# A decoder layer on one core: expert results added in memory by accumulating transfers, a joint way back per tile, a reordered opening

## The reference, cut to what matters

```
x = layernorm(x + self_attention(x))                    # x: 16 x 56 x 256, 16 heads of 16
x = layernorm(x + cross_attention(x, ctx))              # ctx: 16 x 1500 x 256; int8-rounded q and output projections
def ffn(x):                                             # 896 tokens, 8 experts, 2 of them per token
    probs = softmax(x @ gate_w + gate_b)
    weights, selected = top_k(probs, 2); weights /= sum(weights)
    h = gelu(einsum('nd,edf->enf', x, w1) + b1); y = einsum('enf,efd->end', h, w2) + b2
    return einsum('ne,end->nd', comb, y)                # comb holds the two weights of a token
x = layernorm(x + ffn(x))
```

## Time and profile before

| | us |
|---|---|
| median of three runs | 987.98 |
| the profiled execution | 990.07 |
| its span, first to last instruction | 988.1 |

### The profile page before, as it was taken

One profiled execution on the slowest core, in us unless ns is written; L12 is line 12 of the kernel. 1 busy time (PEld: TensorE's weight loads), 2 busy tenths in 40 slices (PEclk: granted clock), 3 DMA queues, 4 the chain that ended last, 5 costly groups with the idle time before them and its releaser, 6 DMA issues.

```text
span 988.1 us, 29769 instructions
## 1 busy us (share of the span) xinstructions
PE 863.9 (87%) x12092; PEld 702.3 (71%) x12093; DVE 623.5 (63%) x1191; ACT 462.0 (47%) x1049; POOL 223.7 (23%) x185
## 2 busy tenths in 40 slices
PE   5759989999999999999999999999987299999950
PEld 3537877787778777777877777787765189988950
DVE  4647676968787877879797877979665411111115
ACT  2316655645565565556555655656554123322310
POOL 4123113212512422152223214222300100000026
PEclk9859999989999999999999999999997589999985
DMA  6424546454644645455455545555538154454523
GB/s 200 134 84 124 151 142 180 122 153 124 188 133 142 185 141 154 146 170 142 151 153 154 158 142 165 147 161 147 190 107 343 56 200 167 171 193 160 170 76 100
DMA packets 98102, 151.32 MB, mean 153 GB/s; under 512 B 12002, under 2 KB 86306, under 8 KB 94144
## 3 DMA queue, kind: packets, MB, share of 16 engines
q1 hardware_dynamic: 96448, 145.40, 47.9%
q0 software_dynamic: 1536, 4.20, 1.3%
HBM read 102.61 MB, written 46.86 MB: 151 GB/s over the span
## 4 chain that ended last, share of the span: by engine, by line
PE 56%; DVE 16%; DMA 11%; ACT 7%; issue 4%; SPq 3%; POOL 2%; DVEq 0%; ACTq 0%
PE ps L1283 9%; PE ps L1290 9%; PE ps L1349 6%; PE ps L1576 6%; PE ps L1588 5%; DVE negmax L445 5%; PE ps L1306 5%; DMA k_dram<-k_two 5%; PE ps L1329 5%; DMA w_sb<-w 3%; PE ps L1358 3%; ACT k_two L1099 3%; DVE k_two L439 2%; ACT pT L1126 2%; DMA k_st<-k_dram 2%
## 5 line engine op out<-in xcount | busy, mean ns | idle before, releaser
L445 DVE TENSOR_REDUCE negmax<-ps 112x1 f32<-112x1500 f32 x128 | 219.3, 1713 | 30.3 <-PE ps L1306 30.1
L1126 ACT ACTIVATE pT<-ps 125x448 f32<-125x448 f32 x384 | 195.5, 547 | 38.0 <-PE ps L1329 34.5
L977 POOL TENSOR_TENSOR ctx_lo<-ctx_raw,ctx_hi 128x1000 fp32r<-128x1000 f32 x47 | 109.7, 2335 | 240.0 <-DVE ctx_hi L430 240.0
L1329 PE MATMUL ps<-qbd,k_st 98*128 98x112 f16 x1536 | 127.4, 216 | 7.2 <-ACT pT L1126 3.6
L1329 PEld LDWEIGHTS ps<-qbd,k_st 98*128 98x128 f16 x1536 | 89.6, 100 | 58.6 <-issue 20.1
L439 DVE SCALAR_TENSOR_TENSOR k_two<-ps,bk_sb,k_two 128x500 f16<-128x500 f32 x96 | 70.8, 738 | 72.0 <-ACT k_two L1099 71.8
L1099 ACT ACTIVATE k_two<-ps,bk_sb 128x500 f16<-128x500 f32 x96 | 65.0, 677 | 89.2 <-PE ps L1283 70.7
L1306 PE MATMUL ps<-k_st,qbd 96*112 96x500 f16 x384 | 104.7, 381 | 0.0
L1082 ACT COPY v_sb<-ps 125x512 f32<-125x512 f32 x96 | 56.3, 586 | 97.9 <-PE ps L1290 97.9
L1237 ACT ACTIVATE hT<-ps,b_col 128x128 f32<-128x128 f32 x168 | 47.9, 368 | 115.2 <-PE ps L1576 115.2
L1349 PE MATMUL ps<-pT,v_sb 125*17 125x56 f32 x6144 | 95.0, 218 | 7.0 <-issue 7.0
(11 more groups left out here) (199 smaller groups left out, 1228.4 us busy)
## 6 DMA issues: line engine op xcount, KB each, us to landing
k_st<-k_dram SPq DMA_DIRECT2D x288, 125.0 KB, 2.6
w_sb<-w SPq DMA_DIRECT2D x29, 1024.0 KB, 4.9
ctx_raw<-ctx_T SPq DMA_DIRECT2D x48, 500.0 KB, 4.5
k_dram<-k_two SPq DMA_DIRECT2D x96, 250.0 KB, 3.4
xs<-zeros SPq DMA_DIRECT2D x28, 256.0 KB, 2.8
ys<-zeros SPq DMA_DIRECT2D x28, 256.0 KB, 2.7
xg<-xs SPq DMA_DIRECT2D x21, 128.0 KB, 4.0
ys<-y_sb SPq DMA_DIRECT2D x21, 128.0 KB, 1.7
```

The lines of the kernel that those rows point to most:

```text
L445: V.tensor_reduce(negmax[0:QW], ps[0:QW, BANK_S:BANK_S + CHUNKS, 0:MC], AX.XY, ALU.max, negate=True).then_inc(max_done, 1)
L977: nc.gpsimd.tensor_tensor(ctx_lo[:, k], ctx_raw[:, k], ctx_hi[:, k].bitcast(F32), ALU.subtract).then_inc(ctx_lo_done, 1)
L1126: nc.scalar.activation(pT[0:MT, (PAIRS * b + p) % 3, TPC * g:TPC * g + TPC], ps[0:MT, BANK_T + n % 2, 0:TPC * QW].rearrange("p (t n) -> p ...
L1329: last = mm(ps[:, BANK_T + n % 2, QW * i:QW * i + QW], k_st[:, j, p, a:a + P], qbd[:, j, p].rearrange("p h s -> p (h s)"), start=True, sto ...
```

## The change

Rows of `xs` become 260 wide: 256 values, then the token's number plus one, the exponential of the gap of its two best logits, and its best expert's number. Routing no longer computes gates or gather slots. x2 is written per tile into a new tensor `sums` (`keep_x2`), and `ys` and its zeroing are gone. In the expert loop VectorE reads the extra columns (`gate`: seven instructions per tile) for the gate, the destination row and b2 times gate; `y_step` gives gate times y plus that; POOL adds the 128 rows into `sums` by one indirect transfer with an add, each waiting for the one before. The row buffer is now reloaded after `gate` has read it, not after the transpose. At the end SP loads `sums` back in four pieces, and ACT normalises tiles 0 to 3, VectorE tiles 4 to 7.

The way back is made once per tile, for both of its batches together, at slot 2 of the even batch and after the last. In the opening the units are spread behind the steps by `FIRST_UNITS`, the last unit goes behind the first scores, the int8 rounding is cut into parts and moved behind steps 4, 7 and 12, wq and wp are loaded ahead of the second context chunk, and some constants move. `o_all` is no longer cleared.

```
-        x1_all = sb("x1_all", [P, TILES, D])
+        rows_all = sb("rows_all", [P, TILES, XW])
+        x1_all = rows_all[:, :, 0:D]
...
+        FIRST_UNITS = {0: (1,), 2: (2,), 4: (3, 4), 5: (5,), 7: (6,), 9: (7, 8), 12: (9,), 14: (10,)}
+        W_GRID, W_INT, W_SCALED = (2, 10), (6, 17), 17
...
-            def o_step(b, par, t):
...
+            def o_step(t):
+                dve.wait_ge(o_back_done, t + 1)
+                o = ps[:, BANK_O, 0:H * VW].rearrange("p (h d) -> p h d", d=VW)
+                V.reciprocal(rsum[:].unsqueeze(2), o[:, :, DH:VW]).then_inc(rsum_done, 1)
+                dve.wait_ge(rsum_done, t + 1)
+                V.tensor_tensor(o_all[:, t].rearrange("p (h d) -> p h d", h=H), o[:, :, 0:DH],
+                                rsum[:].unsqueeze(2).to_broadcast([P, H, DH]), ALU.mult).then_inc(o_read, 1)
+                dve.wait_ge(o_read, t + 1)
+                V.tensor_tensor(o_all[:, t], o_all[:, t], bv_b[:], ALU.add).then_inc(o_done, 1)
...
-                    dve.wait_ge(p_act, t + 1)
-                    V.tensor_scalar(r_den[:], r_exp[:], 1.0, None, ALU.add).then_inc(route, 1)
-                    dve.wait_ge(route, n + 14)
-                    V.reciprocal(comb[:, 0, t:t + 1], r_den[:]).then_inc(route, 1)
-                    dve.wait_ge(route, n + 15)
-                    V.tensor_tensor(comb[:, 1, t:t + 1], r_exp[:], comb[:, 0, t:t + 1], ALU.mult).then_inc(route, 1)
                     if t < TILES - 1:
                         V.tensor_tensor(ohsum[:], ohsum[:], oh16[:], ALU.add).then_inc(route, 1)
-                    dve.wait_ge(route, n + 16)
+                        dve.wait_ge(route, ROUTE * t + 14)
...
-                    elif slot == 2 and not (isinstance(b, int) and b == 0):
-                        o_step(b - 1, 1 - j, t - 1 + j)
+                    elif slot == 2 and b == 0:
+                        row_tails()
+                    elif slot == 2 and j == 0:
+                        o_step(t - 1)
...
+            unit_step(0, 0, 0)
             for k in range(A_STEPS):
-                if k < UNITS:
-                    unit_step(0, 0, k)
-                if k == 3:
-                    ctx_hi_step(0, 0, 2)
-                elif k == 8:
-                    ctx_hi_step(1, 1, 0)
                 a_step(k, 0)
                 a_tail(k, 0)
                 if k == 2:
                     kbd_part(0)
-                elif k == 3:
+                elif k == 4:
+                    ctx_hi_step(0, 0, 2)
+                    dve.wait_ge(w_nat_in, 32)
+                    weights_grid(0)
+                    weights_int8(0)
+                elif k == 7:
+                    weights_grid(1)
+                elif k == 10:
                     dve.wait_ge(small_in, 16 * len(SMALL))
-                    weights_to_int8(0)
-                elif k == 5:
-                    weights_to_int8(1)
-                elif k == 7:
+                elif k == 12:
+                    weights_int8(1)
+                elif k == 13:
+                    ctx_hi_step(1, 1, 0)
+                for u in FIRST_UNITS.get(9 if k == 10 else k if k != 9 else -1, ()):
+                    unit_step(0, 0, u)
             max_step(0, 0)
             row_halves(0, 0)
+            unit_step(0, 0, 11)
...
+            def gate(g):
+                row, q = xg[:, g % 2], g % 4
+                one = slice(q, q + 1)
+                e = dve.value_load(e_tab[0:1, g:g + 1], min_val=0, max_val=E - 1)
+                V.scalar_tensor_tensor(g_num[:, one], row[:, D + 2:D + 3], e_sum[:, g:g + 1], row[:, D + 1:D + 2],
+                                       ALU.is_equal, ALU.max).then_inc(gate_step, 1)
+                V.tensor_scalar(g_den[:, one], row[:, D + 1:D + 2], 1.0, None, ALU.add).then_inc(gate_step, 1)
+                V.tensor_scalar(g_spare[:, one], row[:, D:D + 1], 0.5, p_back[:, 2:3], ALU.is_lt, ALU.mult).then_inc(gate_step, 1)
+                dve.wait_ge(gate_step, 5 * g + 3)
+                V.scalar_tensor_tensor(g_token[:, one], row[:, D:D + 1], -1.0, g_spare[:, one], ALU.add, ALU.max).then_inc(row_read, 1)
+                V.reciprocal(g_rec[:, one], g_den[:, one]).then_inc(gate_step, 1)
+                dve.wait_ge(gate_step, 5 * g + 4)
+                V.tensor_tensor(g_gate[:, one], g_num[:, one], g_rec[:, one], ALU.mult).then_inc(gate_step, 1)
+                dve.wait_ge(gate_step, 5 * g + 5)
+                V.tensor_scalar(g_b2[:, q], b2_all[:, bass.ds(e, 1)].rearrange("p a n -> p (a n)"), g_gate[:, one], None,
+                                ALU.mult).then_inc(gate_done, 1)
+            def y_step(g):
+                q = g % 4
+                dve.wait_ge(gate_done, g + 1)
                 dve.wait_ge(m2_done, g + 1)
-                if not (isinstance(n, int) and n == 0):
-                    dve.wait_ge(y_out[par], 16 * n)
-                V.tensor_tensor(y_sb[:, par], ps[:, Y_BANK + par, 0:D], b2_all[:, bass.ds(e, 1)].rearrange("p a n -> p (a n)"),
-                                ALU.add).then_inc(y_ready, 1)
...
+            gate(0)
+            gate(1)
+            for g in range(GT):
+                if g + 2 < GT:
+                    xgT_step(g + 2, g % 2)
+                y_step(g)
+                if g + 2 < GT:
+                    gate(g + 2)
...
+            for half in range(2):
+                tiles = range(4 * half, 4 * half + 4)
+                for t in tiles:
+                    dve.wait_ge(sum_in[t // 2], 16)
+                    V.bn_stats(st8[:, t], acc[:, t]).then_inc(f_stat, 1)
...
+            for n, src in enumerate((wq, wp)):
+                sp.dma_start(w_nat[n], src[:]).then_inc(w_nat_in, 16)
             load_ctx(0, 0, 1, True)
             for dst, src in SMALL:
...
+            def keep_x2(t, kept):
+                sp.wait_ge(b_x2_kept, kept)
+                sp.dma_start(sums_tiles[bass.ds(t, 1)].rearrange("a p n -> (a p) n"),
+                             acc[:, bass.ds(t, 1)].rearrange("p a n -> p (a n)")).then_inc(sums_set, 16)
...
-                        if u in (0, 2, 8, 11):
-                            q = (0, 2, 8, 11).index(u)
-                            clear(*((xs_rows, xs_zeroed), (ys_rows, ys_zeroed))[j], it, q)
+                        if u in (0, 2, 8, 11) and j == 0:
+                            clear(xs_rows, xs_zeroed, it, (0, 2, 8, 11).index(u))
+                        if u == 2 and j == 1 and not first:
+                            keep_x2(it - 1, it)
...
-                    sp.wait_ge(tx_done, read)
+                    sp.wait_ge(row_read, read)
                 sp.dma_start(xg[:, par], xs_tiles[rows].rearrange("a p n -> (a p) n")).then_inc(xg_in[par], 16)
-            def store_y(g, par):
-                rows = row_tile(g)
-                sp.wait_ge(y_ready, g + 1)
-                sp.dma_start(ys_tiles[rows].rearrange("a p n -> (a p) n"), y_sb[:, par]).then_inc(y_out[par], 16)
             sp.wait_ge(p_dve, at["rows known"])
...
+            sp.dma_start(b2_all[:], b2.unsqueeze(0).to_broadcast([P, E, D])).then_inc(b2_in, 16)
             load_xg(2, 0, 1)
-            sp.dma_start(b2_all[:], b2.unsqueeze(0).to_broadcast([P, E, D])).then_inc(b2_in, 16)
             with sp.Fori(0, (GT - 3) // 2) as it:
                 for par in range(2):
                     load_w1(2 * it + 2 + par, par, 4 * it + 2 + 2 * par)
                     load_xg(2 * it + 3 + par, 1 - par, 2 * it + 2 + par)
-                    store_y(2 * it + par, par)
             load_w1(GT - 1, 0, 2 * GT - 4)
-            for g in range(GT - 3, GT):
-                store_y(g, g % 2)
+            sp.wait_ge(added, 16 * GT)
+            for q in range(TILES // 2):
+                sp.dma_start(acc[:, 2 * q:2 * q + 2], sums_tiles[2 * q:2 * q + 2].rearrange("t p n -> p t n")).then_inc(sum_in[q], 16)
             for t in range(TILES):
-                sp.wait_ge(f_out, t + 1)
+                sp.wait_ge(f_out[t // 4], t % 4 + 1)
...
-            pool.wait_ge(y_out[0], 16 * (GT - GT // 2))
-            pool.wait_ge(y_out[1], 16 * (GT // 2))
...
-            for t in range(TILES):
-                for k in range(2):
-                    nc.gpsimd.indirect_dma_start(
-                        out=got[:, k, t], out_offset=None, in_=ys,
-                        in_offset=bass.IndirectOffsetOnAxis(ap=slot_gather[:, t, k:k + 1], axis=0)).then_inc(gathered[t], 16)
...
+            pool.wait_ge(sums_set, 16 * (TILES + 1))
+            for g in range(GT):
+                pool.wait_ge(row_read, g + 1)
+                pool.wait_ge(y_ready, g + 1)
+                if g > 0:
+                    pool.wait_ge(added, 16 * g)
+                nc.gpsimd.indirect_dma_start(
+                    out=sums, out_offset=bass.IndirectOffsetOnAxis(ap=g_token[:, g % 4:g % 4 + 1], axis=0),
+                    in_=y_sb[:, g % 2], in_offset=None, compute_op=ALU.add).then_inc(added, 16)
...
+            act.wait_ge(f_mean, 1)
+            act.wait_ge(f_rstd, 1)
+            for t in range(4):
```

(40 more changed lines are left out.)

263 lines of the change are left out of this document (131 added, 132 removed).

## The result

The kernel after takes 954.76 us (median of 4 runs, 951.91 to 957.26), the one before beside it 988.95 (4 runs, 987.93 to 992.11). The ratio is 0.965, with a 95% interval of 0.961 to 0.968. The forecast was 963 in a range of 952 to 975. The profiled execution took 955.01 for a span of 953.1; that span is 35.0 shorter than the one of before.

A forecast was written before the change was run, and what follows sets the result against it. PE was taken to bound attention and the expert loop, no engine the opening, and PE idles at the end. Terms -8 - 4 + 1.7 + 1.3 - 4.8 - 10.8 = -24.6 from 987.98 gave 963.4 us, range 952 to 975.

The forecast's parts named there:

- more than I count: Rival: batches 0 to 2 at full clock (4 to 5), odd batches short as even, -4 more; near 955; chance 0.17.
- Opening: Up to first scores: two weight roundings and a key-load wait leave the chain, -10.6; with added costs, net -8 us.
- one of the forecast's own signs of being wrong: Opening: the prediction is wrong if the chain of waits there goes through the moved key units; no size given.
- Attention: Odd batches lose four zero writes of 256 KB; half of 1.2 us for seven batches, -4 us, bounds -9 and +2.
- Gates off VectorE: Routing beside attention: L614 would wait in L612's place for POOL's subtraction, so three removed instructions count for nothing.
- Tail: Last way back, behind batch 15: +3.2 us, less 1.5 saved at batch 15's slot 2; net +1.7, bounds 0 and +3.2.
- It doubles: Last way back, behind batch 15: 32 more instructions, taking 3.17 us there, so +3.2 us.
- Start of the expert stage: Row tile 2's load waits for the first gate, behind the second tile's transpose step and b2's landing: +1.3 us.
- Loop: Expert loop: the store of y leaves SP, w1 is issued 3 to 5 us earlier; 17 x 0.28 = -4.8 us.
- The adding transfer: Indirect transfer with add, per expert tile and at the end: 4.0 us to landing, hidden in the loop up to 6.5.
- the rival's mechanism: Expert loop: adding transfers above 6.5 us set the pace of 21 tiles, slower than before from 7.6 us; chance 0.05.
- End: From the last y to the end: adding transfers, four loads, statistics and 16 outputs replace 16 gathers, -10.8 us.

The follow-up runs named there:

- the second profile of the kernel after: The changed kernel run once more, unchanged, beside three edited ones: 955.5 us, ratio 0.964 to the kernel before.
- the last kernel: Changed kernel with a later wait for b2, rows of 272 instead of 260 elements and 8 output transfers instead of 16: 950.35 us, ratio 0.962.
- e3_store_later: Kernel before with SP's store of y issued one tile later, behind the next loads of w1 and rows: 985.14 us, ratio 0.997.
- The plain transfer: Changed kernel with the add left out of the indirect transfers, so results are written over the rows: 953.78 us, ratio 0.963.
- The second transfer: Changed kernel with a plain scatter of the same rows behind each adding one, waited for before the next tile's: 1000.1 us, no ratio.

## Why the prediction was right, and where its terms were off

The time is inside the range, and the three big terms (opening, loop, end) have their sign and their size. The forecast was 8 us too careful, outside its own 959 to 967, and the number came out where the rival "more than I count" had it, near 955, though of that rival only the clock's part came, and half of that. In four smaller ones (attention, gates, tail, start of the experts) a step failed. Term by term, against the ledger:

**Opening: -8 forecast, -10.2 measured to the first scores, and -2.1 more in batch 0.** The chain of waits of the kernel after, with pieces that answer to the earlier trace rows:

```profile
8.83 5.66 DMA ctx_raw<-ctx_T
...
41.07 1.13 PE ps L1472 x4
...
51.26 0.70 DVE q_st L558
...
52.65 1.42 PE ps L1347 x12
...
54.06 0.65 PE ps L1363 x3
```

No rounding of weights and no load of `k_st` stands in it, as forecast. But one of the forecast's own signs of being wrong did come: the chain goes through the moved units. Their matmuls (L1340, L1347) are 15.4 us of it, where the same lines (L1283, L1290) were 7.9 before, and one unit, the 1.42 us at 52.65, stands right ahead of the first scores. So PE's units have filled part of the time that came free.

The added cost was sized too high in one place: the later context chunk lands at 14.49 instead of 13.92, 0.6 for the 1.9 I charged. The rest of the difference is not separated; the clock is part of it. The granted clock was 0.86 up to the first max before and is 0.97 after, and batch 0 went from 0.90 to 1.00. In batch 0 that was the rival "more than I count", worth 4 to 5, and about half came. A full clock isn't owned by the change: in the kernel with 8 output transfers 10.2 us at the low level (1.2 GHz) fell into the opening, and the first scores came at 58.2:

```profile
0.00:58.20 58.20, 37.49 (x179) 28.05 (x181) 33.41 (x61) 14.09 (x27) 14.72 (x25) 0.91 0.53 157
```

**Attention: -4 forecast, -4.7 measured in batches 1 to 14; the cause was wrong, and the match is luck.** Against the second profile of the kernel after, the same stretch gives -0.9. I put it on the zero writes that odd batches lose. Writing them again lengthens the odd batches by 1.2 us in all, with more low clock in them (what is left of the 4 us is inside the noise of the totals), and the kernel with only the way back keeps all of them and has the short batch 1. My reading of the earlier trace rows took a difference between odd and even batches for something that the zero writes do; batches lean on each other, and where one cuts them decides which is long (from max to max, the even ones are the longer ones). What was gained in every profile is batch 1, which lost its neighbour's way back. In batches 2 to 13 the joint way back frees 11.5 us of PE and nothing of it arrives: PE's time without work grows from 23.1 to 33.3. The even batches among them got longer, by 3 us with the joint way back alone and 5 to 9 with the whole change. What holds them in PE's place is not settled. The chain of waits runs through the landing of `k_dram`, which is longer in most kernels with the joint way back (a median of 3.6 to 4.1 us, against 3.4 to 3.5). But in the last kernel it is 3.2, and these batches take the same 533.7. The low clock blurs the rest: the profiles have between 0 and 17 us of it in these batches, and the three longest sums (541.7, 537.5 and 536.0) have 17.1, 10.2 and 6.8. Among profiles that have 6.8 us there, the two without the joint way back take 534.4 and 535.0, the four with it 531.9 to 536.0.

**Gates off VectorE: 0 forecast, for a reason that failed.** I had L614 take over L612's wait. After, the long instruction is simply gone, and L614's successor, L621, takes 150 ns. L639, another long one that becomes L646, did not take it over either; it was long already (VectorE's lines, the first of before: busy us, mean ns):

```profile
L639 DVE TENSOR_TENSOR b_y<-b_y,x_all 128x256 f32<-128x256 f32 x8 | 15.4, 1931 | 0.3
...
L646 DVE TENSOR_TENSOR b_y<-b_y,rows_all 128x256 f32<-128x256 f32 x8 | 13.4, 1680 | 0.3
...
L621 DVE TENSOR_TENSOR ohsum<-ohsum,oh 128x8 bf16<-128x8 bf16 x7 | 1.0, 150 | 0.0
```

The timelines say why L621 is free. Before, L612 starts 0.15 us behind POOL's subtraction and ends with it. After, with three instructions less ahead of it, L621 has come and gone when the subtraction starts:

```profile
596.71 2.32 POOL L977 TENSOR_TENSOR ctx_lo<-ctx_raw,ctx_hi 128x1000 fp32r<-128x1000 f32 x1 [0.75 <-DVE ctx_hi L430]
...
596.86 2.19 DVE L612 TENSOR_TENSOR comb<-r_exp,comb 128x1 f32<-128x1 f32 x1
```

```profile
221.41 0.15 DVE L621 TENSOR_TENSOR ohsum<-ohsum,oh 128x8 bf16<-128x8 bf16 x1
...
221.63 2.33 POOL L1017 TENSOR_TENSOR ctx_lo<-ctx_raw,ctx_hi 128x1000 fp32r<-128x1000 f32 x1 [0.75 <-DVE ctx_hi L444]
```

It is so in all six tiles beside attention. The step that failed is "will start inside the same subtraction"; that VectorE's instruction is held when it does start inside stands. So VectorE has some 13 us less to do, and the time shows nothing of it that can be told. The forecast was right by the wrong argument.

**Tail: +1.7 forecast, -1.9 measured (-1.5 in batch 15, -0.4 behind it).** "It doubles" is the step that failed: the 64 instructions take the time of 32, 3.17 us, as shown above. The saving of 1.5 in batch 15 is not shown: against the second profile it is 1.0, and the kernel with the opening alone, which has no joint way back, is 0.7 shorter there too.

**Start of the expert stage: +1.3 forecast, +1.2 measured between the first and the third `m1`** in this profile (15.7 us for 14.5), but -0.1 in the second (14.4), and +1.9 and +1.1 from the last reciprocal to the first y. The forecast had the gate behind `xgT_step(1)`; what held it here was b2 (timeline of the kernel after):

```profile
782.01 0.22 DVE L797 SCALAR_TENSOR_TENSOR g_num<-xg,e_sum 128x1 f32<-128x1 f32 x1 [2.00 <-DMA b_all<-b]
...
782.78 0.33 SPq L969 DMA_DIRECT2D xg<-xs  x1
...
784.79 0.44 PE L1311 MATMUL ps<-id,xg 128*128 128x128 f32 x2 [0.82 <-DMA xg<-xs]
```

The gate comes 2 us later than `xgT` allows, and the load of rows takes 2.0 instead of the 4.0 that I took from a median; the two errors cancel, which is luck. In the second profile b2 landed 1.5 us sooner after its issue, the gate did not wait for it, and nothing was lost.

**Loop: -4.8 forecast, -4.8 measured.** Order on SP, nothing else (e3_store_later). After, SP issues a load of w1 as soon as the `m1` that read the buffer has ended, at 872.73. It is for the next `m1` but one, which starts 10.6 us later, where before had 5.0, and PE waits for nothing:

```profile
869.00 3.73 PE L1639 MATMUL ps<-xgT,w_sb 128*128 128x128 f32 x32
...
872.91 0.33 SPq L957 DMA_DIRECT2D w_sb<-w  x1
876.25 3.73 PE L1639 MATMUL ps<-xgT,w_sb 128*128 128x128 f32 x32
...
883.49 3.73 PE L1639 MATMUL ps<-xgT,w_sb 128*128 128x128 f32 x32
```

The working has a slip that changes nothing: 935.00 to 942.24 is one step, not two, and its 7.24 us are right.

**The adding transfer: 4.0 forecast, 3.8 measured, and hidden.** The plain transfer gives the same loop, so there is no trace of the rival. The second transfer shows that the rival's mechanism is real once the chain is longer than a tile. (Its break-even was off by a little: 21 x 1.1 and 7 are 30, and the 24.6 are used up from about 7.4 us on, not from 7.6.) By the Trainium skill (Collectives: The Full Stack, section The bandwidth ceiling: the fold count and why AG ≠ RS ≠ AR) the add was to be paid in doubled reads, 5.6 us by my estimate. The measured 3.8 against 2.6 shows less than a doubling at this size.

**End: -10.8 forecast, -12.5 measured.** The forecast's chain stands in the timeline step by step:

```profile
928.24 1.55 POOL L1112 DMA_INDIRECT sums<-y_sb,g_token  x1 [5.47 <-DVE y_sb L816]
...
932.77 1.55 POOL L1112 DMA_INDIRECT sums<-y_sb,g_token  x1 [2.98 <-DMA sums<-y_sb,g_token]
936.59 1.94 SPq L987 DMA_DIRECT2D rows_all<-sums  x4
939.41 1.44 DVE L836 BATCH_NORM_STATS2 st<-rows_all 128x6 f32<-128x256 f32 x4 [8.47 <-DMA rows_all<-sums]
...
944.17 1.69 ACT L1303 ACTIVATE o_all<-o_all,sm 128x256 f32<-128x256 f32 x4
944.69 6.81 SPq L991 DMA_DIRECT2D out<-o_all  x16
```

From one adding transfer to the next are 4.5 us (forecast 4.6), from the last y's end to the statistics 8.5 (8.6), to the first output 13.8 (14.4), to the end 22.2 (23.8). Each step came a little under its term.

## What to carry to other kernels

A store that waits for a result, queued ahead of the next load on the same queue, delays that load by the whole wait; issuing it one step later, or on another engine's queue as in the kernel after, gave 4.8 us of 988 for nothing. Work that is taken from the busiest engine is not time until its waits have been read too: here 11.5 us of PE and 23 of VectorE vanished, and the stretch was 1.3 us shorter in one profile and 1.6 longer in the other. A difference between odd and even steps of a schedule names no cause; put the suspected cost back into the new kernel and look. And a term that fits in one profile is not yet right: two terms here matched in the first profile and not in the second of the same kernel.

## What the hardware showed that I had not expected

Matmuls of 17 columns that write output partitions 0 to 55 and 64 to 119 in turn run two for the time of one: 64 in 1.83 us, 32 in 1.82, the two of a pair 6 to 7 ns apart. A VectorE add of two tiles of 128 x 256 that started 0.22 us behind a POOL subtraction took 2.43 us and ended with it; started 0.14 us ahead of one, it took 0.42. An indirect transfer with an add holds POOL for 1.55 us instead of 0.95 and lands 1.2 us later. The same plain one landed in 2.6 us ahead of a load of 1 MB, in 4.2 to 5.2 behind its issue, and in 2.4 with no such load. Zero writes of rows of 1088 bytes landed sooner (2.8 us) than those of 1040 bytes (3.3); with 1024 bytes, before, it was 2.8.
